# A two-layer graph network on one core: block bases loaded one per slice, packs of the next block in its free places, indices of the small group kept, and chunks 0 to 3 ahead of the last two

## The chip, the cores and the metric

The kernel runs on one core of a Trainium2 chip. The metric is the device time of one execution in microseconds (us), the median over several. The cores have these engines: TensorE (PE in the profile; PEld are its weight loads), VectorE (DVE), ScalarE (ACT), GpSimd (POOL) and SyncE (SP), which here only issues DMAs. A "q" behind an engine's name is its sequencer.

## The reference

There are 12500 nodes with 128 features, and 200000 edges, sorted by their destination `dst`, with a random source `src` and 64 edge features. Small destinations are far more frequent than large ones.

```python
def _dmpnn_layer(x, src, dst, edge_attr, W_msg, Wih, Whh, bih, bhh):
    msg = jnp.concatenate([x[src], edge_attr], axis=-1) @ W_msg.T
    agg = jax.ops.segment_sum(msg, dst, num_segments=n_nodes)
    return _gru_cell(agg, x, Wih, Whh, bih, bhh)

h = jnp.maximum(_layernorm(x, axis=-1), 0.0)
x = x + layer2(layer1(h))
```

`_gru_cell(m, h, ...)` makes r and z by sigmoids of two sums of matrix products, n by a tanh, and gives (1 - z) * n + z * h. All numbers are float32.

## The kernel before

**The edges.** They go in groups of 512 (128 partitions by 4 tiles): 390 full ones and a rest of 320 edges on 80 partitions, called the small group or the rest group. For a group, VectorE compares the destinations with a lane of numbers to make `onehot` (L1130), and TensorE multiplies it with the edge features (L786, in layer 0 only) and with the rows of the source nodes (L802), which gives sums for a window of 80 nodes in PSUM. VectorE adds the window to `edgeT` (L1192) and `aggT` (L1195), at a base that it reads from a table with a value load (L1187). `onehot` is made two places ahead.

**Two kinds of groups.** For 288 full groups and the rest, the source rows are gathered by GpSimd, four indirect DMAs of L666 a group, into a ring of six buffers. The first 102 groups have the smallest destinations. Their rows aren't gathered: TensorE builds count matrices out of one-hots (`lo_hot` L1108 and `v_hot` L1115, both of VectorE; matmuls of L755), ScalarE copies them to `a_blk` (L1385), and TensorE multiplies them with the resident node rows (L762) in seven slices. A count matrix of a slice is made in four packs.

**The block loop.** In each layer a loop of 12 blocks (`ITERS`) runs over 24 gathered groups (`gi` 0 to 23) in each block; in layer 0 every fourth place holds one dense group for its edge features alone, 32 places in all. Slice `sl` takes the groups 3 `sl` to 3 `sl` + 2, its phases 0 to 2. In phase 0 VectorE makes the one-hots of packs 2 and 3, in phase 2 those of packs 0 and 1 of the next slice, and in phase 2 of the last slice (`gi` = 20) those of packs 0 and 1 of the next block. In phase 1 of the last slice it prepares the next block. At `gi` = 21 TensorE turns the sums of the block's dense tiles into five short windows (L832), and `add_block` on VectorE reads five bases (L1217) and makes five adds (L1224).

**The chunks.** When all edges of 250 nodes are added, their GRU is computed as one of 50 chunks. The functions of L411 to L417 run the chunks that are ready behind `gi` = 5, 11 and 17 and behind the block's last place; L419 to L424 run all that are left behind the rest group. Both are loops at run time, with bounds that the kernel reads from a table. TensorE's part of a chunk is L866 to L895 (it begins with L875 and L879), ScalarE's L1418 to L1460, VectorE's L1269 to L1291. ScalarE also issues the chunk's DMAs: the store (L1420) and in layer 1 a load (L1448). `chunk_at` (L426) turns the place in the order into a chunk's number, computed in registers where it is used: on TensorE for L879, on ScalarE for L1420, L1429, L1448 (layer 1) and L1455 (layer 0). The order before is 4, 5, ..., 49, 0, 1, 2, 3, as the blocks' dense tiles reach into the nodes of chunks 0 to 3 until the last block; `late` makes these four ready at the very end. So chunk 48 is the last one in the loop, and 49, 0, 1, 2, 3 stand behind the rest group.

**What sets the order.** Each engine's program is written out; engines wait for each other by semaphores. SP issues the loads of edge features, destinations and indices in the order of use, each behind a wait for a free buffer (L513). Its load of the rest group's indices (L592) comes last in a layer. GpSimd's gathers of a layer begin when every row of its table is stored (L662). The registers' value loads are TENSOR_LOAD and FUSED_REGOPS in the profile.

```python
c = i + ROT - CHUNKS * ((i + ROT + 64 - CHUNKS) >> 6)
...
base = dve.value_load(base_i[0:1, bass.ds(g, 1)], min_val=0, max_val=N)
added_before(p)
dve.wait_ge(group_summed, p + (layer * ORDERED[0] + 1 + AHEAD))
...
starts = [dve.value_load(window_base[0:1, bass.ds(it * NR + r, 1)], min_val=0, max_val=N) for r in range(NR)]
```

Of the kernel before, what the change touches and what calls it, by code (L numbers as in the profile page):

```python
# [7 lines left out]
I32 = mybir.dt.int32  # L8
# [5 lines left out]
P = 128  # L14
# [18 lines left out]
SLOTS = SUBS * RING  # L33
ROT = 4
AR = 4
REGIONS = ((8, 2, 14), (7, 3, 20), (8, 4, 32), (7, 5, 36), (4, 6, 26))
# [14 lines left out]
def build(nc, x, src, dst, edge_attr, weights, h_table, x1_table, out):  # L51
# [5 lines left out]
    GROUPS = FULL + 1  # L57
    CHUNKS = N // CHUNK
    NT = N // QUART
    LN_STEPS = CHUNKS // LN_C  # L60
# [26 lines left out]
    with ctx:  # L87
# [28 lines left out]

        idx = sb("idx", [P, IDX_RING, RING, TILES], I32)
        dst_in = sb("dst_in", [P, AR, TILES], I32)
        rel = sb("rel", [P, 2, TILES])
# [56 lines left out]
        ones = start_only(P, 1)  # L176
        late = start_only(P, 1)
        need = start_only(P, 1)
# [73 lines left out]
        rows_loaded = [sem(f"rows_loaded{s}") for s in range(RING)]  # L252
        hr_loaded = [sem(f"hr_loaded{k}") for k in range(SUBS)]
        gather_issued = sem("gather_issued")
        dst_rows_loaded = sem("dst_rows_loaded")
# [114 lines left out]
        def idx_use(layer, it, gi):  # L370

            u, r = divmod(gi, RING)
            return it * (SUBS // IDX_RING) + u // IDX_RING + layer * (STEPS // IDX_RING + (u % IDX_RING == 0 and r == 0))

# [51 lines left out]
        def chunk_at(i):  # L426

            if isinstance(i, int):
                return (i + ROT) % CHUNKS
            c = i + ROT - CHUNKS * ((i + ROT + 64 - CHUNKS) >> 6)  # L430
            return nc.s_assert_within(c, 0, CHUNKS - 1,
                                      skip_runtime_bounds_check_because="a place plus ROT modulo the number of chunks")

# [62 lines left out]
        def _(sp):  # L496
# [54 lines left out]
            for layer in range(2):  # L551
# [3 lines left out]
                for gi in range(RING):  # L555
                    load_idx(0, gi)
                if layer == 0:
                    for p in range(AR):
                        load_edges(0, DENSE - HEAD + p, p)
                    for i in range(LN_STEPS):  # L560
                        sp.wait_ge(ln_relu, i + 1)
                        for a, b in PARTS:
                            sp.dma_start(by_node(h_table)[a:b, i * LN_C:(i + 1) * LN_C, :],
                                         hr_chunks(i * LN_C, (i + 1) * LN_C)[a:b]).then_inc(h_stored, 16)
                    for p in range(AR, HEAD):
                        slot_free(0, p)
                        load_edges(0, DENSE - HEAD + p, p % AR)
                else:
                    for q, gi, ai in order(layer)[:AR]:
                        load_group(layer, 0, q, gi, ai)  # L570
                    sp.wait_ge(out_stored, 16 * CHUNKS)
                    for k in range(SUBS):
                        first, last = ((slice_at[min(2 * i, SLICES)] + NQ - 1) // NQ for i in (k, k + 1))
                        for a, b in PARTS:
                            sp.dma_start(hr_chunks(first, last)[a:b],
                                         by_node(x1_table)[a:b, first:last, :]).then_inc(hr_loaded[k], 16)
# [14 lines left out]

                sp.dma_start(idx[0:REST, 0, 0, :], edges(src, FULL, REST)).then_inc(idx_loaded[0][0], 16)  # L592
                for k in range(2):
# [10 lines left out]
        def _(pool):  # L604
# [9 lines left out]
            nc.gpsimd.iota(bend[:, :], pattern=[[1, STEPS]], base=1, channel_multiplier=0, **small)  # L614
            nc.gpsimd.memset(late[:, :], float(STEPS + 1)).then_inc(late_made, 1)
            nc.gpsimd.memset(zero[:, :], 0.0)
# [17 lines left out]
            for r, (n, w, c) in enumerate(REGIONS):  # L634
                nc.gpsimd.affine_select(out=row_of[:, tiles_of(r)], in_=row_of[:, tiles_of(r)], compare_op=ALU.is_ge, fill=0.0,
                                        base=ROW_AT[r] + w - 1, pattern=[[w, n]], channel_multiplier=-1)
            pool.wait_ge(late_made, 1)
            nc.gpsimd.affine_select(out=late[:, :], in_=late[:, :], compare_op=ALU.is_ge, fill=0.0,
                                    base=-(CHUNKS - ROT - 1), pattern=[[0, 1]], channel_multiplier=1)
            pool.wait_ge(ident_zeroed, 1)  # L640
# [16 lines left out]
            for layer in range(2):  # L657
# [5 lines left out]

                def gather(s, i, parts):
                    for j in range(TILES):
                        nc.gpsimd.indirect_dma_start(  # L666
                            out=rows[0:parts, s, j, :], out_offset=None, in_=table[:, :],
                            in_offset=bass.IndirectOffsetOnAxis(ap=idx[0:parts, i, s, j:j + 1].bitcast(U32), axis=0),
                        ).then_inc(rows_loaded[s], 16)
# [7 lines left out]
                with pool.Fori(0, ITERS) as it:  # L677
                    for gi in range(SLOTS):
# [4 lines left out]
                        pool.sem_inc(gather_issued, 1)  # L683
                        gather(r, i, P)
                pool.wait_ge(group_summed, layer * ORDERED[0] + place(layer, ITERS, rows_free(0)) + 1 + AHEAD)
                pool.wait_ge(idx_loaded[0][0], (idx_use(layer, ITERS, 0) + 1) * 16)
                pool.sem_inc(gather_issued, 1)
                gather(0, 0, REST)

# [242 lines left out]
        def _(dve):  # L932
# [13 lines left out]
            for c in range(LN_STEPS + 1):  # L946
# [15 lines left out]
                if c >= 1:  # L962
# [37 lines left out]
            dve.wait_ge(consts_made, 1)  # L1000
            nc.vector.scalar_tensor_tensor(out=touch[:, :], in0=max_all[:, :], scalar=float(ROT * CHUNK),
                                           in1=gidx[:, :], op0=ALU.is_ge, op1=ALU.mult)
# [7 lines left out]
            chained(nc.vector.tensor_scalar(over[:, 0:1], over[:, 0:1], WIN - 0.5, None, ALU.is_ge))  # L1010
            chained(nc.vector.tensor_tensor(need[:, :], need[:, :], late[:, :], ALU.max))

# [110 lines left out]
            for layer in range(2):  # L1123
# [90 lines left out]

                def add_block(it, blk, p):

                    starts = [dve.value_load(window_base[0:1, bass.ds(it * NR + r, 1)], min_val=0, max_val=N) for r in range(NR)]  # L1217
                    added_before(p)
# [92 lines left out]
                with dve.Fori(0, ITERS) as it:  # L1311
                    blk = block_of(layer, it)
                    for q, gi, ai in order(layer):
                        g = it * ATTR + ai if gi is None else gathered(it, gi)
                        add_window(place(layer, it, q), g, slot(layer, q), P, gi is not None)
                        onehot_after(it, q)
                        if gi == USED:
                            add_block(it, blk, place(layer, it, q + 1))
                        if gi is not None and gi < USED:
# [6 lines left out]
                            elif phase == 2 and sl + 1 < SLICES:  # L1326
                                for k in range(2):
                                    pack_of(blk, sl + 1, k)
                            elif phase == 2:
                                for k in range(2):  # L1330
                                    lo_pack(it + 1, k)
                                    pack_of(blk + 1, 0, k)
                            elif sl == SLICES - 1:
                                prepare(it + 1)
                                nc.vector.tensor_scalar(v_onehot[:, :], lane[0:VC, :], vrel[:, bass.ds(it, 1)], None,
                                                        ALU.is_equal).then_inc(v_hot_made, 1)
# [173 lines left out]
```

## Time and profile before

| | |
|---|---|
| median of 3 runs | 3290.52 us (3289.2 to 3294.56) |
| the profiled execution | 3279.4 us, span 3277.7 us, mean granted TensorE clock 0.835 |
| layer 0: first and last gather | 73.0 to 1666.7 us |
| chunks behind the rest group of layer 0 | 1685.7 to 1718 us |
| layer 1: gathers | 1723.1 to 3221.7 us |
| chunks behind the rest group of layer 1 | 3238.8 to 3277.7 us |

Times are read from the start of the span. A row of a timeline gives start, duration, engine, line, operation, tiles and shapes, and in brackets how long the engine sat idle before it and what released it; "issue" is time in which it waited for nothing that the profile shows (its sequencer was at other instructions). A wait is listed with its sum, its count and its longest. The clock is given as a share of 2.4 GHz: 1.00 and 0.50 are the two levels.

### The profile page before, as it was taken

The numbers are of one execution on the slowest core, as the hardware profiler recorded it, in microseconds if no ns is written. First come the engines' busy times: TensorE is split into PE (matmuls) and PEld (weight loads), VectorE is DVE, ScalarE is ACT, GpSimd is POOL, SyncE is SP. The second block draws the span as 40 slices with busy tenths as digits, with TensorE's granted clock in tenths as the row PEclk, the third lists the DMA queues.
The fourth block names the chain that finished last, engine by engine and source line by source line (L and its number), as shares of the span: only waits on it lengthen the run. The fifth ranks groups of instructions, "written<-read, shape, count | busy, mean of one in ns | idle before, by whom it ended". The sixth has DMA issues, their size and how long they took to land.

```text
span 3277.7 us, 74395 instructions
## 1 busy us (share of the span) xinstructions
PE 2630.1 (80%) x20375; PEld 2360.7 (72%) x20376; DVE 1530.0 (47%) x4895; ACT 999.1 (30%) x2343; POOL 2324.6 (71%) x2389
## 2 busy tenths in 40 slices
PE   0689889899898898898975777787787787787887
PEld 0578778788787787787855676687677677686675
DVE  5544455454454544545443444444444445444444
ACT  5212223232232333332341222232232233333333
POOL 4477777777777776776717777777777777777772
PEclk9988798798798898988986777777787787887888
DMA  7233333333333333333315222222222222222221
GB/s 195 56 88 86 86 94 90 85 94 88 87 93 88 85 91 82 92 80 80 88 33 128 54 55 58 56 62 55 61 59 58 60 63 60 64 60 62 65 61 43
DMA packets 350922, 249.44 MB, mean 76 GB/s; under 512 B 226506, under 2 KB 312334, under 8 KB 350628
## 3 DMA queue, kind: packets, MB, share of 16 engines
q0 software_dynamic: 75232, 155.02, 17.5%
q1 hardware_dynamic: 254617, 70.47, 10.3%
q10 hardware_dynamic: 20779, 20.48, 2.1%
q8 instruction: 130, 2.13, 0.3%
q14 instruction: 164, 1.34, 0.1%
HBM read 226.51 MB, written 19.20 MB: 75 GB/s over the span
## 4 chain that ended last, share of the span: by engine, by line
PE 35%; POOL 30%; issue 16%; DVE 6%; DVEq 4%; DMA 3%; ACT 3%; ACTq 1%; SPq 1%; POOLq 1%
POOL rows L666 30%; PE ps_v L762 9%; PE ps_win L802 8%; PE ps_win L786 4%; PE ps_q L755 3%; DVEq L1187 2%; PE ps_c L755 2%; PE ps_b L879 1%; PE ps_b L880 1%; PE ps_d L866 1%; PE ps_d L895 1%; ACT hr L1366 1%; PE ps_a L886 1%; DVEq L1217 1%; PE ps_c L888 1%
## 5 line engine op out<-in xcount | busy, mean ns | idle before, releaser
L666 POOL DMA_INDIRECT rows<-h_table,idx x1156 | 1153.2, 998 | 485.3 <-issue 376.2
L666 POOL DMA_INDIRECT rows<-x_table,idx x1156 | 1144.5, 990 | 410.4 <-issue 402.1
L802 PE MATMUL ps_win<-onehot,rows 128*128 128x80 f32 x4624 | 743.3, 312 | 202.5 <-DMA rows<-x_table,idx 162.8
L802 PEld LDWEIGHTS ps_win<-onehot,rows 128*128 128x128 f32 x4624 | 663.7, 221 | 248.7 <-issue 145.9
L762 PE MATMUL ps_v<-hr,a_blk 125*128 125x128 f32 x4800 | 715.2, 319 | 0.0
L762 PEld LDWEIGHTS ps_v<-hr,a_blk 125*128 125x128 f32 x4800 | 698.4, 235 | 0.8
L1385 ACT COPY a_blk<-ps_q 125x224 f32<-125x224 f32 (+5 forms) x504 | 223.8, 480 | 856.3 <-PE ps_q L755 763.7
L1115 DVE SCALAR_TENSOR_TENSOR v_hot<-v_cur,lane 128x42 bf16<-128x42 f32 (+13 forms) x1180 | 435.1, 425 | 0.0
L786 PE MATMUL ps_win<-onehot,attr 128*64 128x80 f32 x3128 | 312.2, 253 | 120.2 <-DVE onehot L1130 80.4
L755 PE MATMUL ps_q<-v_hot,lo_hot 128*125 128x28 bf16 (+5 forms) x3696 | 289.4, 222 | 139.9 <-DVE v_hot L1115 117.7
L755 PEld LDWEIGHTS ps_q<-v_hot,lo_hot 128*125 128x125 bf16 x3696 | 272.5, 151 | 151.2 <-DVE v_hot L1115 128.9
L786 PEld LDWEIGHTS ps_win<-onehot,attr 128*64 128x64 f32 x3128 | 258.7, 149 | 158.0 <-DVE onehot L1130 77.8
L1195 DVE TENSOR_TENSOR aggT<-aggT,ps_win 128x80 f32 x578 | 133.0, 230 | 499.4 <-PE ps_win L802 436.7
L1130 DVE TENSOR_TENSOR onehot<-lane,rel 128x320 f32<-128x320 f32 x682 | 338.2, 496 | 23.4
L1192 DVE TENSOR_TENSOR edgeT<-edgeT,ps_win 64x80 f32 x391 | 89.6, 229 | 453.9 <-PE ps_win L802 286.6
L1385 ACT ACT_TABLE_LOAD x96 | 123.2, 1283 | 364.7 <-PE ps_q L755 348.4
L1280 DVE SCALAR_TENSOR_TENSOR r_sb<-ps_a,bT,r_sb 128x250 f32<-128x250 f32 x100 | 47.8, 478 | 362.5 <-ACT r_sb L1450 292.0
L1385 ACT COPY a_blk<-ps_c 125x70 f32<-125x70 f32 (+7 forms) x672 | 208.3, 376 | 15.1 <-PE ps_c L755 11.1
L755 PE MATMUL ps_c<-v_hot,lo_hot 128*125 128x70 bf16 (+3 forms) x2016 | 200.3, 244 | 6.5 <-DVE v_hot L1115 6.5
L755 PEld LDWEIGHTS ps_c<-v_hot,lo_hot 128*125 128x125 bf16 x2016 | 167.9, 158 | 11.8 <-DVE v_hot L1115 8.0
L1127 DVE TENSOR_SCALAR rel<-dst_in,base_all 128x4 f32<-128x4 int32 x682 | 163.5, 240 | 7.8 <-issue 6.4
L1442 ACT COPY h_ch<-ps_a 128x250 f32<-128x250 f32 x100 | 36.6, 366 | 383.7 <-PE ps_a L875 383.4
(191 smaller groups left out, 2038.3 us busy)
## 6 DMA issues: line engine op xcount, KB each, us to landing
attr<-in_edge_attr_dram SPq DMA_DIRECT2D x390, 128.0 KB
rows<-h_table,idx POOLq DMA_INDIRECT x1156
rows<-x_table,idx POOLq DMA_INDIRECT x1156
dst_in<-in_dst_dram SPq DMA_DIRECT2D x678, 2.0 KB
idx<-in_src_dram SPq DMA_DIRECT2D x576, 2.0 KB
x_table<-out_sb ACTq DMA_DIRECT2D x50, 125.0 KB
attr<-in_x_dram ACTq DMA_DIRECT2D x50, 125.0 KB
out_dram<-out_sb ACTq DMA_DIRECT2D x50, 125.0 KB
```

Of the source, the lines that this page charges most:

```text
L666: nc.gpsimd.indirect_dma_start(out=rows[0:parts, s, j, :], out_offset=None, in_=table[:, :], in_offset=bass.IndirectOffsetOnAxis(ap=idx[0: ...
L755: mm = nc.tensor.matmul((ps_q, ps_c)[k % 2][0:QUART, own], lo_hot[:, t + j, :], v_hot[:, k % 2, own], start=True, stop=True)
L762: mm = nc.tensor.matmul(ps_v[0:VC, 0:H], a_blk[:, t - slice_at[sl], :], hr[:, t, :], start=(t == 0), stop=(t == NT - 1))
L786: mm = nc.tensor.matmul(ps_win[r % 2][0:D, WIN:2 * WIN], attr[0:parts, r, j, :], onehot[0:parts, r % 2, j, :], start=(j == 0), stop=(j == ...
L802: mm = nc.tensor.matmul(ps_win[r % 2][:, 0:WIN], rows[0:parts, rr, j, :], onehot[0:parts, r % 2, j, :], start=(j == 0), stop=(j == TILES - 1))
L1115: ins = nc.vector.scalar_tensor_tensor(out=v_hot[:, k % 2, at].rearrange("p (t c) -> p t c", c=wide), in0=cur[:, t:t + n].unsqueeze(2).to_ ...
L1127: nc.vector.tensor_scalar(rel[:, s % 2, :], dst_in[:, s, :], float(N), base_all[:, bass.ds(g, 1)], ALU.min, ALU.subtract).then_inc(rel_rea ...
L1130: nc.vector.tensor_tensor(onehot[:, s % 2, :, :], lane[:, 0:WIN].unsqueeze(1).to_broadcast([P, TILES, WIN]), rel[:, s % 2, :].unsqueeze(2) ...
L1187: base = dve.value_load(base_i[0:1, bass.ds(g, 1)], min_val=0, max_val=N)
L1192: ins = nc.vector.tensor_tensor(e, e, ps_win[s % 2][0:D, WIN:2 * WIN], ALU.add)
L1195: ins = nc.vector.tensor_tensor(a, a, ps_win[s % 2][:, 0:WIN], ALU.add)
L1385: ins = nc.scalar.copy(a_blk[:, 0:hs, row:row + n * w].rearrange("p h (j w) -> p j h w", w=w), (ps_q, ps_c)[k % 2][0:QUART, at].rearrange( ...
```

## The change

The five bases of a block's windows are read one each in phase 1 of slices 0 to 4 and kept in registers until `add_block`. The one-hots of packs 0 and 1 of the next block are made behind groups 22 and 23, one pack each, where both stood behind group 20. The rest group's indices have a tile of their own, loaded once at the start, and GpSimd waits for that. Chunks 0 to 3 stand ahead of chunks 48 and 49: order 4, ..., 47, 0, 1, 2, 3, 48, 49. For that `early` and `cap` take the place of `late` in the small computation at the start that finds when a chunk is ready, and `chunk_at` has three shifts where it had one.

```diff
+LAST = 2
+    MOVED = CHUNKS - ROT - LAST
+        idx_rest = sb("idx_rest", [P, TILES], I32)
...
-            return it * (SUBS // IDX_RING) + u // IDX_RING + layer * (STEPS // IDX_RING + (u % IDX_RING == 0 and r == 0))
+            return it * (SUBS // IDX_RING) + u // IDX_RING + layer * (STEPS // IDX_RING)
...
         def chunk_at(i):
             if isinstance(i, int):
-                return (i + ROT) % CHUNKS
-            c = i + ROT - CHUNKS * ((i + ROT + 64 - CHUNKS) >> 6)
+                return i + ROT if i < MOVED else i - MOVED if i < MOVED + ROT else i
+            c = i + ROT - (MOVED + ROT) * ((i + 64 - MOVED) >> 6) + MOVED * ((i + 64 - MOVED - ROT) >> 6)
+            c = c - CHUNKS * ((i + 64 - CHUNKS) >> 6)
...
                 if layer == 0:
+                    sp.dma_start(idx_rest[0:REST, :], edges(src, FULL, REST)).then_inc(rest_loaded, 16)
                     for p in range(AR):
...
-                sp.dma_start(idx[0:REST, 0, 0, :], edges(src, FULL, REST)).then_inc(idx_loaded[0][0], 16)
...
-            nc.gpsimd.memset(late[:, :], float(STEPS + 1)).then_inc(late_made, 1)
+            nc.gpsimd.iota(cap[:, :], pattern=[[1, 1]], base=CHUNK, channel_multiplier=CHUNK, **small)
+            nc.gpsimd.memset(early[:, :], float(ROT * CHUNK)).then_inc(late_made, 1)
...
-            nc.gpsimd.affine_select(out=late[:, :], in_=late[:, :], compare_op=ALU.is_ge, fill=0.0,
-                                    base=-(CHUNKS - ROT - 1), pattern=[[0, 1]], channel_multiplier=1)
+            nc.gpsimd.affine_select(out=early[:, :], in_=early[:, :], compare_op=ALU.is_ge, fill=0.0,
+                                    base=MOVED - 1, pattern=[[0, 1]], channel_multiplier=-1)
...
-                pool.wait_ge(idx_loaded[0][0], (idx_use(layer, ITERS, 0) + 1) * 16)
+                pool.wait_ge(rest_loaded, 16)
                 pool.sem_inc(gather_issued, 1)
-                gather(0, 0, REST)
+                gather(0, idx_rest, REST)
...
-            nc.vector.scalar_tensor_tensor(out=touch[:, :], in0=max_all[:, :], scalar=float(ROT * CHUNK),
+            chained(nc.vector.tensor_scalar(cap[:, :], cap[:, :], float((CHUNKS - LAST) * CHUNK), None, ALU.max))
+            nc.vector.tensor_tensor(cend[:, :], cend[:, :], cap[:, :], ALU.min)
+            nc.vector.scalar_tensor_tensor(out=touch[:, :], in0=max_all[:, :], scalar=early[:, 0:1],
                                            in1=gidx[:, :], op0=ALU.is_ge, op1=ALU.mult)
...
-            chained(nc.vector.tensor_tensor(need[:, :], need[:, :], late[:, :], ALU.max))
...
-                def add_block(it, blk, p):
-
-                    starts = [dve.value_load(window_base[0:1, bass.ds(it * NR + r, 1)], min_val=0, max_val=N) for r in range(NR)]
+                def add_block(starts, blk, p):
+
...
                         if gi == USED:
-                            add_block(it, blk, place(layer, it, q + 1))
+                            add_block(starts, blk, place(layer, it, q + 1))
+                        if gi is not None and gi > USED and gi - USED <= 2:
+                            lo_pack(it + 1, gi - USED - 1)
+                            pack_of(blk + 1, 0, gi - USED - 1)
...
-                            elif phase == 2:
-                                for k in range(2):
-                                    lo_pack(it + 1, k)
-                                    pack_of(blk + 1, 0, k)
-                            elif sl == SLICES - 1:
+                            elif phase == 1 and sl < NR:
+                                starts.append(dve.value_load(window_base[0:1, bass.ds(it * NR + sl, 1)], min_val=0, max_val=N))
+                            elif phase == 1 and sl == SLICES - 1:
                                 prepare(it + 1)
```

## Rows read from the trace of the kernel before

**Rows 1.** The page: part 1, busy us and share; part 4, the chain by line.

```profile
PE 2630.1 (80%) x20375; PEld 2360.7 (72%) x20376; DVE 1530.0 (47%) x4895; ACT 999.1 (30%) x2343; POOL 2324.6 (71%) x2389
...
POOL rows L666 30%; PE ps_v L762 9%; PE ps_win L802 8%; PE ps_win L786 4%; PE ps_q L755 3%; DVEq L1187 2%; PE ps_c L755 2%; PE ps_b L879 1%; PE ps_b L880 1%; PE ps_d L866 1%; PE ps_d L895 1%; ACT hr L1366 1%; PE ps_a L886 1%; DVEq L1217 1%;
```

**Rows 2.** Windows: us from:to, length, busy of each engine, PEclk, DMA share, GB/s.

```profile
862.00:1662.00 800.00, 719.78 (x5911) 633.75 (x5910) 396.49 (x1269) 264.92 (x624) 570.31 (x575) 0.89 0.34 86
1723.00:3221.00 1498.00, 1162.19 (x8464) 1065.22 (x8464) 653.08 (x1932) 434.58 (x1004) 1143.85 (x1156) 0.78 0.26 63
1252.20:1262.40 10.20, 7.45 (x23) 5.10 (x24) 3.04 (x11) 1.11 (x3) 7.76 (x9) 0.50 0.25 67
854.00:862.00 8.00, 4.58 (x27) 4.04 (x28) 2.42 (x10) 0.00 (x0) 6.17 (x7) 0.64 0.37 90
```

**Rows 3.** Waits of PE, 1723 to 3221: us, times, longest.

```profile
PE ps_win L802 <- DMA rows<-x_table,idx: 162.8, 69, 16.7
```

**Rows 4.** Waits of PE, 862 to 1662.

```profile
PE ps_win L786 <- DVE onehot L1130: 42.4, 29, 5.1
PE ps_win L786 <- issue: 18.9, 6, 3.8
PE ps_q L755 <- DVE v_hot L1115: 5.2, 18, 0.5
PE ps_b L879 <- issue: 3.8, 19, 0.3
```

**Rows 5.** Instructions of L879, 862 to 1662: duration ns, first and last start.

```profile
L879 PE MATMUL ps_b<-aggT,wT x60: 374/473/782, 866.1 to 1641.0; 128*128 x60
```

**Rows 6.** Timeline of DVE, end of block 9: start, us, instruction, [idle before].

```profile
1240.47 2.04 DVE L1108 TENSOR_TENSOR lo_hot<-lane,lo_t 128x1000 bf16<-128x1000 f32 x2
...
1243.85 0.65 DVE L1115 SCALAR_TENSOR_TENSOR v_hot<-v_cur,lane 128x70 bf16<-128x70 f32 x2
...
1246.73 0.49 DVE L1130 TENSOR_TENSOR onehot<-lane,rel 128x320 f32<-128x320 f32 x1
1250.51 0.17 DVE L1224 TENSOR_TENSOR aggT<-aggT,ps_v 128x14 f32 x1 [3.28 <-issue]
...
1256.20 0.23 DVE L1192 TENSOR_TENSOR edgeT<-edgeT,ps_win 64x80 f32 x1 [0.40 <-issue]
```

**Rows 7.** Instructions of L1217: duration ns min/median/max.

```profile
L1217 DVEq FUSED_REGOPS  x240: 57/132/190, 228.6 to 3221.1; - x120
L1217 DVEq TENSOR_LOAD <-edgeT x120: 298/300/318, 228.8 to 3220.7; - x120
```

**Rows 8.** Timeline of PE, end of block 9.

```profile
1254.21 1.33 PE L786 MATMUL ps_win<-onehot,attr 128*64 128x80 f32 x8 [5.11 <-DVE onehot L1130]
...
1256.93 1.20 PE L879 MATMUL ps_b<-aggT,wT 128*128 x2
...
1273.18 1.32 PE L786 MATMUL ps_win<-onehot,attr 128*64 128x80 f32 x8 [3.77 <-issue]
```

**Rows 9.** Timeline of POOL, end of layer 0.

```profile
1662.19 0.91 POOL L666 DMA_INDIRECT rows<-h_table,idx  x1 [13.36 <-DMA idx<-in_src_dram]
```

**Rows 10.** Timeline of PE, end of layer 0.

```profile
1680.64 1.12 PE L802 MATMUL ps_win<-onehot,rows 80*128 80x80 f32 x8
1685.68 0.65 PE L875 MATMUL ps_a<-ident,h_rows 125*128 125x125 f32 x2 [3.92 <-issue]
```

**Rows 11.** Instructions of L1420: duration ns min/median/max.

```profile
L1420 ACTq FUSED_REGOPS  x98: 172/184/193, 306.8 to 3268.5; - x98
```

**Rows 12.** Timeline of all engines, around a chunk in mid-block.

```profile
1201.74 0.47 ACT L1457 ACTIVATE z_sb<-ps_d,b_gate 128x250 f32<-128x250 f32 x1 [0.19 <-PE ps_d L895]
...
1205.64 0.28 PE L786 MATMUL ps_win<-onehot,attr 128*64 128x80 f32 x1 [0.57 <-DVE onehot L1130]
```

**Rows 13.** Timeline of PE, end of layer 1.

```profile
3264.22 0.69 PE L895 MATMUL ps_d<-m_sb,wT 128*128 128x250 f32 x2 [0.23 <-ACT r_sb L1450]
```

**Rows 14.** Waits of all engines, 3221 to 3278.

```profile
PE ps_b L879 <- DVE aggT L1195: 5.7, 1, 5.7
```

More of the change, by code:

```diff
@@ L176, in build @@
         ones = start_only(P, 1)
-        late = start_only(P, 1)
+        early = start_only(P, 1)
+        cap = start_only(P, 1)
         need = start_only(P, 1)
@@ L253, in build @@
         hr_loaded = [sem(f"hr_loaded{k}") for k in range(SUBS)]
+        rest_loaded = sem("rest_loaded")
         gather_issued = sem("gather_issued")
@@ L428, in chunk_at @@
             if isinstance(i, int):
-                return (i + ROT) % CHUNKS
-            c = i + ROT - CHUNKS * ((i + ROT + 64 - CHUNKS) >> 6)
+                return i + ROT if i < MOVED else i - MOVED if i < MOVED + ROT else i
+            c = i + ROT - (MOVED + ROT) * ((i + 64 - MOVED) >> 6) + MOVED * ((i + 64 - MOVED - ROT) >> 6)
+            c = c - CHUNKS * ((i + 64 - CHUNKS) >> 6)
             return nc.s_assert_within(c, 0, CHUNKS - 1,
-                                      skip_runtime_bounds_check_because="a place plus ROT modulo the number of chunks")
+                                      skip_runtime_bounds_check_because="the first ROT chunks stand behind all but the last LAST")
         def edges(a, g, parts):
@@ L662, in _, with gather @@
                     pool.wait_ge(out_stored, 16 * CHUNKS)
-                def gather(s, i, parts):
+                def gather(s, at, parts):
                     for j in range(TILES):
@@ L667, in gather @@
                             out=rows[0:parts, s, j, :], out_offset=None, in_=table[:, :],
-                            in_offset=bass.IndirectOffsetOnAxis(ap=idx[0:parts, i, s, j:j + 1].bitcast(U32), axis=0),
+                            in_offset=bass.IndirectOffsetOnAxis(ap=at[0:parts, j:j + 1].bitcast(U32), axis=0),
                         ).then_inc(rows_loaded[s], 16)
@@ L683, in _ @@
                         pool.sem_inc(gather_issued, 1)
-                        gather(r, i, P)
+                        gather(r, idx[:, i, r, :], P)
                 pool.wait_ge(group_summed, layer * ORDERED[0] + place(layer, ITERS, rows_free(0)) + 1 + AHEAD)
-                pool.wait_ge(idx_loaded[0][0], (idx_use(layer, ITERS, 0) + 1) * 16)
+                pool.wait_ge(rest_loaded, 16)
                 pool.sem_inc(gather_issued, 1)
-                gather(0, 0, REST)
+                gather(0, idx_rest, REST)
                 def over_gather(g, parts, sent, n, done):
@@ L1312, in _ @@
                     blk = block_of(layer, it)
+                    starts = []
                     for q, gi, ai in order(layer):
```

## The prediction

> **What bounds the kernel now.** I read the page first: TensorE is busy 80% of the span and GpSimd 71% [rows 1], so no engine bounds the whole. Next the windows by stage. From 862 to 1662 us, the second half of layer 0, TensorE's records fill 719.8 of 800 us; from 1723 to 3221, the groups of layer 1, they fill 78% of it while GpSimd is busy 1143.85 of 1498 us in 1156 transfers [rows 2]. The list of waits then says what ends TensorE's idle time. In layer 1 it is the gathered rows, 162.8 us [rows 3]: there GpSimd's pace sets the time. In 862 to 1662 no wait for rows is in the list. What is there is 42.4 us for `onehot` (longest 5.1), 18.9 us of "issue" (the jump back of the block loop, up to 3.8 each time), 5.2 us for `v_hot` in 18 waits and 3.8 us before L879 in 19 [rows 4]. So in blocks 6 to 11 of layer 0 every microsecond that TensorE loses or gains is one of the end. Those are six block ends, 30 chunks (60 matmuls of L879, two per chunk [rows 5]), 18 of them the first of a step in mid-block, six the first at a block end, six the second of a step.
>
> A profiled execution took 3279.4 us against a median of 3290.5, 11.1 less; the sum is made on the profiled one and its difference laid on the median. A measurement of this kernel tells about 0.2%, 6.6 us, from no change.
>
> **Part A and B, the block's end.** [Rows 6] are VectorE's records of one. At gathered group 20 (counted from 0) two packs take it from 1240.47 to the end of the `v_hot` of 1243.85, some 3.95 us. Then `onehot` at 1246.73, then 3.28 us of idle under "issue" before the first add of L1224: the five value loads of L1217. One load holds the sequencer 0.71 us: a TENSOR_LOAD of 0.30, register instructions of 0.06 and 0.19, the gaps between them [rows 7]; five make 3.55. TensorE waits 5.11 us for the onehot behind them, and its chunk, L879 at 1256.93, begins 0.73 after VectorE's last add at 1256.20 [rows 6, 8]. Moved to phase 1 of slices 0 to 4, each load lies in idle time of VectorE (busy half the stretch [rows 2]), and I cost it at nothing; were that cover gone, the five would cost 3.55 again. The packs, 3.95 us, are not saved: they stand behind the onehots of groups 22 and 23 instead, 2.6 and 1.35, still ahead of the last add. With the onehots first, TensorE's wait of 5.1 shrinks to about 0.8, and VectorE makes packs while TensorE multiplies the last groups; but the last add, and with it L879, still waits for all of VectorE's work. So of that path the 3.28 us go, and about 0.8 come back where VectorE waits for the matmuls of the last groups: gain 2.5 us an end, bounds 1.5 (if more comes back) and 3.3 (nothing does). Six ends in the bound stretch: **−15 us** (−9 to −20). The next block's first matmuls come at 1273.18 [rows 8], 16 us later, so the packs are not late. In layer 1 and in blocks 0 to 5 rows are waited for: nothing.
>
> **Part C, the rest's indices.** The load moves to the start, one more DMA on SP there, beside hundreds of loads. GpSimd no longer waits for it at the end of a layer; in layer 0 that wait is 13.36 us [rows 9]. Its first transfer goes at 1662.19 [rows 9]; TensorE takes the group at 1680.64, behind chunk 48 [rows 10]. Nothing, bounds 0 and −1.
>
> **Part D, the order.** Before: chunk 48, rest group, then chunks 49, 0, 1, 2, 3. After: 0, 1, 2, 3, 48, rest group, 49. Six chunks either way behind the last group, one jump of 3.9 us either way [rows 10], one chunk at the low clock ahead of it and one behind. SP loads layer 1's attributes when the rest group is summed, now some 20 us later; the first gather of layer 1 needs every chunk stored and comes later still. Nothing by itself, bounds ±2. The one more iota and one more small VectorE instruction at the start run before the turned tiles arrive: nothing.
>
> **What D costs: the chunk's index.** A chunk's number is computed from a loop register wherever it is used. Before this is one FUSED_REGOPS with one shift, 184 ns on ScalarE's L1420 [rows 11]; after it has three shifts, four multiplications and about eight sums. The shortest of L1217, a multiply and two sums, take 57 ns [rows 7], so the shift and two cheap operations more are 127 ns, most of it the shift. Two more shifts at about 0.1 and eight cheap operations at about 0.01 give an extra δ of 0.27 us for each use. Bounds: 0.1 if only the cheap ones count, 0.4 if the whole triples. I take 0.27, as the row with the same operations is nearest.
> How often is it on the path? [Rows 12] show a chunk in mid-block. TensorE computes it before L879 (+δ). ScalarE computes it before its store L1420, then its L1450, then before the copies L1429 and L1455: these stand one behind the other on its sequencer, so L1457 moves by 4δ less its slack of 0.19, then VectorE's last three operations, its next value load, add and onehot, and TensorE, which already waits 0.57 us for that onehot. So a first chunk in mid-block costs 4δ − 0.19 = 0.89, 18 times: 16.0. The six second chunks cost about 2δ, 3.2; the six at block ends δ, 1.6. Sum **+21 us** in the stretch.
> The tails: six chunks of layer 0's end at δ, +1.6. In layer 1's end TensorE waits for ScalarE's L1450 before L895 [rows 13], behind two DMAs each with its index: 2δ for four chunks and δ for the two at the low clock, +2.7; its block end, where L879 waits 5.7 us for the adds [rows 14], gives back 1.5.
> As layer 0 saturates a little earlier and layer 1's last blocks wait for rows by under 1 us, +2.
>
> Sum: −15 + 20.8 + 1.6 + 2.7 − 1.5 + 2 = **+10.6**, 3290.0 on the profiled execution, **3301 us** on the median. In δ: 106δ − 3.4 − 14.5; nothing is gained or lost at δ = 0.17, a gain over 6.6 us needs δ under 0.11.
>
> The row of a TENSOR_LOAD is 0.30 us and its whole load 0.71 [rows 7]. The Trainium skill (Runtime: NRT & Kernel Launch, "Instruction fetch mechanics") puts such a load at about 200 ns for each register; by that five loads would be 1.0 us, A would give little, and the sum would be near +24. The trace disagrees with it here, as the idle time that it ends is 3.28.
>
> **Rivals.**
> 1. The index is cheap, δ = 0.1. For it: the added operations are mostly sums and products. Against: the one shift seems the dear part. Then 106δ = 10.6, and the sum is −7.3: 3283 us, faster. It decides from δ under 0.11. Chance 0.17.
> 2. The clock. After the 5.1 us stall TensorE stood at 0.50 for 10.2 us with 7.45 us busy [rows 2], the 1.2 GHz level. If a stall of 0.8 plus one of 3 us keeps 2.4 GHz, half of the 7.45 goes at six ends, −22 us: 3279 us. Against: TensorE still idles some 3.6 us in all before L879, and shorter waits at 856 us were also followed by a low clock (0.64 in the mean of 854 to 862 [rows 2]). Chance 0.12.
> 3. Neither is on the path: GpSimd's transfers pace layer 0 too, and its slack takes both. Then only the tails remain, +3: 3293 us. Against: no wait for rows after 862. Chance 0.12.
> 4. The moved packs and loads hit a busy VectorE: the gain is 0 to 1 an end instead of 2.5: +20 to +25, 3312 us. Chance 0.09.
> 5. D does not do what it says: chunks 0 to 3 don't become ready before the last groups and the order is as before. The time would be that of the forecast, since D by itself is worth nothing.
>
> **How the numbers follow.** The forecast, with δ between 0.2 and 0.35, has 0.50; its own range is 3294 to 3308. The range from 3276 to 3312 takes in rivals 1, 3 and most of 2. Faster by over 0.2% is below 3283.9: rival 2 and half of rival 1, with spread 0.24. Slower is above 3297.1: most of the forecast and rival 4, 0.50. The same: 0.26.
>
> **What would show it.** Idle before L1224 falls from 3.28 to under 0.3 and the five value loads stand one each at gathered groups 1, 4, 7, 10 and 13; TensorE's longest wait for onehot in a block falls from 5.1 to about 1, with a new wait before L879 of about 3 us; FUSED_REGOPS of L1420, L1429, L1448, L1455 and L879 grow from 0.18 to 0.45; the wait for onehot after a mid-block chunk grows from 0.57 to about 1.4; layer 1's chunks behind the rest group come about 0.5 us further apart. FUSED_REGOPS still under 0.3, or a clock of 1.00 behind the block end, would make the forecast wrong.

## The result

The changed kernel takes 3308.08 us in the median of 7 executions (3296.66 to 3321.07), the kernel before 3289.2 in 7 beside it (3279.99 to 3294.56). The ratio is 1.0067, with a 95% interval of 1.0052 to 1.0083: by that 22 us slower (the two medians differ by 19), where 10.6 were forecast, and 3308 against a forecast of 3301 in a range of 3276 to 3312. Single executions of one kernel lie up to 25 us apart. The profiled one of the changed kernel took 3321.07 us, 13 above its median, while the one of before was 11 below its own. So the two traces differ by 42 us where the kernels differ by 22, and a trace is read here for what a step does, not for the total.

The profile page of the changed kernel, its first part and the row of the granted clock:

```profile
PE 2669.9 (80%) x20375; PEld 2392.0 (72%) x20376; DVE 1530.4 (46%) x4896; ACT 1011.6 (30%) x2343; POOL 2336.5 (70%) x2390
...
PEclk9988888898798897888986677787787787787887
```

The same 20375 matmuls take 40 us more than in [rows 1]. No matmul was added, and the mean granted clock is 0.824 where it was 0.835, which is about that much. The waits of TensorE from 862 to 1690 us (the same six blocks as in [rows 4], which take longer here):

```profile
PE ps_win L793 <- DVE onehot L1138: 20.7, 24, 1.1
PE ps_b L886 <- DVE edgeT L1200: 20.2, 6, 3.6
PE ps_win L793 <- issue: 19.5, 6, 3.7
PE ps_b L886 <- issue: 10.8, 24, 0.6
PE ps_a L882 <- issue: 7.0, 6, 1.2
PE ps_q L762 <- DVE v_hot L1123: 4.5, 13, 0.5
```

Beside [rows 4] the wait for `onehot` has fallen from 42.4 us to 20.7 and its longest from 5.1 to 1.1. In its place stands a new wait of up to 3.6 us, 20.2 in all, at the six block ends, where L886 (L879 before) waits for the last add, and the "issue" in front of L886 has grown from 3.8 to 10.8 us. VectorE at the end of block 9, first, TensorE, second, and third TensorE's first row there in the kernel before:

```profile
1264.37 0.49 DVE L1138 TENSOR_TENSOR onehot<-lane,rel 128x320 f32<-128x320 f32 x1
1264.78 0.16 DVE L1231 TENSOR_TENSOR aggT<-aggT,ps_v 128x14 f32 x1
...
1268.33 2.04 DVE L1116 TENSOR_TENSOR lo_hot<-lane,lo_t 128x1000 bf16<-128x1000 f32 x2
...
1271.88 0.87 DVE L1116 TENSOR_TENSOR lo_hot<-lane,lo_t 128x125 bf16<-128x125 f32 x2
1272.67 0.64 DVE L1123 SCALAR_TENSOR_TENSOR v_hot<-v_cur,lane 128x70 bf16<-128x70 f32 x2
1273.23 0.22 DVE L1200 TENSOR_TENSOR edgeT<-edgeT,ps_win 64x80 f32 x1
```

```profile
1263.45 0.43 PE L839 MATMUL ps_v<-v_onehot,v_rows 128*128 128x128 f32 x2
...
1268.47 0.77 PE L793 MATMUL ps_win<-onehot,attr 128*64 128x80 f32 x8 [1.10 <-DVE onehot L1138]
1270.33 0.40 PE L882 MATMUL ps_a<-ident,h_rows 125*128 125x125 f32 x2 [1.09 <-issue]
1274.32 1.20 PE L886 MATMUL ps_b<-aggT,wT 128*128 x2 [3.58 <-DVE edgeT L1200]
```

```profile
1243.92 0.43 PE L832 MATMUL ps_v<-v_onehot,v_rows 128*128 128x128 f32 x2
```

The first add has no idle time in front of it; in [rows 6] it was 3.28 us. But both packs now stand between the block's adds and the last add, and TensorE waits for that. From the block's own matmul (L839) to L886 it is 10.87 us; before it was 13.01, from 1243.92 to the 1256.93 of [rows 8].

The index of the store on ScalarE, which was one FUSED_REGOPS of 184 ns in [rows 11]:

```profile
L1429 ACTq FUSED_REGOPS  x294: 42/184/223, 305.6 to 3309.5; - x147
```

There are three for each of the 98 stores: one of about 184 ns, one of about 218 and one of about 48. From a store's first register instruction to its DMA it is 0.351 us before and 0.599 here, in the median of the 98. So the δ of the prediction is 0.25. TensorE's register instructions have no records, but its idle time in front of the chunk's L886 grew from 0.17 to 0.44. All engines around a chunk in mid-block, and under them the first matmul of the chunk of [rows 12] in the kernel before:

```profile
1206.41 0.38 PE L882 MATMUL ps_a<-ident,h_rows 125*128 125x125 f32 x2
1207.23 0.68 PE L886 MATMUL ps_b<-aggT,wT 128*128 x2 [0.44 <-issue]
...
1211.97 0.47 ACT L1466 ACTIVATE z_sb<-ps_d,b_gate 128x250 f32<-128x250 f32 x1
...
1213.84 0.42 DVE L1298 TENSOR_TENSOR z_sb<-m_sb,r_sb 128x250 f32<-128x250 f32 x1
...
1215.99 1.25 PE L793 MATMUL ps_win<-onehot,attr 128*64 128x80 f32 x8 [0.85 <-DVE onehot L1138]
```

```profile
1196.87 0.38 PE L875 MATMUL ps_a<-ident,h_rows 125*128 125x125 f32 x2
1197.41 0.68 PE L879 MATMUL ps_b<-aggT,wT 128*128 x2 [0.17 <-issue]
```

L1466 no longer waits for TensorE: ScalarE's own sequencer is late. From the chunk's first matmul (1206.41) to L793 it is 9.58 us; before, it was 8.77 (1196.87 to the 1205.64 of [rows 12]). TensorE's wait for the onehot behind it is 0.85 us; the prediction had 1.4. And then something follows that the kernel before doesn't show here. Windows of the changed kernel, and under them those of the kernel before, at about the same place: the second of each pair begins some 0.5 us behind the start of L793 (0.4 behind that of L786 before). The clock is the third number from the end:

```profile
1206.00:1215.00 9.00, 8.55 (x69) 6.71 (x67) 2.24 (x6) 3.21 (x9) 6.87 (x8) 1.00 0.31 81
1216.50:1226.50 10.00, 10.00 (x59) 9.59 (x58) 5.45 (x19) 2.14 (x7) 7.56 (x9) 0.51 0.30 75
```

```profile
1197.00:1206.00 9.00, 8.27 (x69) 6.55 (x68) 3.02 (x8) 4.16 (x9) 6.87 (x8) 1.00 0.34 95
1206.00:1216.00 10.00, 9.73 (x98) 9.06 (x97) 6.29 (x22) 2.47 (x8) 7.56 (x9) 1.00 0.31 78
```

Behind a wait of 0.85 us TensorE fell to 1.2 GHz for 10 us and did 59 matmuls in a stretch that held 98 before, behind a wait of 0.57.

### The profile page after: what moved, and what is told of

It is laid out like the page before. It is cut to its first block, busy times and chain, and to the rows that moved or that the text cites. A ratio compares the mean times of both kernels' runs of the same rounds, so it can differ in the third digit from the quotient of the medians.

```text
span 3319.4 us, 74786 instructions
## 1 busy us (share of the span) xinstructions
PE 2669.9 (80%) x20375; PEld 2392.0 (72%) x20376; DVE 1530.4 (46%) x4896; ACT 1011.6 (30%) x2343; POOL 2336.5 (70%) x2390
## 4 chain that ended last, share of the span: by engine, by line
PE 41%; POOL 25%; issue 15%; DVE 6%; ACT 3%; DMA 3%; ACTq 3%; DVEq 2%; SPq 1%; POOLq 0%
POOL rows L673 25%; PE ps_v L769 12%; PE ps_win L809 10%; PE ps_win L793 5%; PE ps_q L762 3%; PE ps_c L762 2%; PE ps_b L886 2%; PE ps_b L887 2%; DVEq L1195 2%; ACTq L1429 1%; PE ps_d L873 1%; DMA rows<-x_table,idx 1%; ACT hr L1375 1%; DVE v_hot L1123 1%; PE ps_a L893 1%
## 5 line engine op out<-in xcount | busy, mean ns | idle before, releaser
L809 PE MATMUL ps_win<-onehot,rows 128*128 128x80 f32 x4624 | 753.8, 315 | 195.6 <-DMA rows<-x_table,idx 157.4
L809 PEld LDWEIGHTS ps_win<-onehot,rows 128*128 128x128 f32 x4624 | 674.1, 224 | 241.9 <-issue 124.8
L769 PE MATMUL ps_v<-hr,a_blk 125*128 125x128 f32 x4800 | 723.4, 321 | 0.0
L769 PEld LDWEIGHTS ps_v<-hr,a_blk 125*128 125x128 f32 x4800 | 706.5, 237 | 0.7
L793 PE MATMUL ps_win<-onehot,attr 128*64 128x80 f32 x3128 | 313.5, 253 | 79.4 <-DVE onehot L1138 45.3
L793 PEld LDWEIGHTS ps_win<-onehot,attr 128*64 128x64 f32 x3128 | 259.6, 149 | 116.2 <-issue 59.7
L1135 DVE TENSOR_SCALAR rel<-dst_in,base_all 128x4 f32<-128x4 int32 x682 | 165.3, 242 | 10.6 <-issue 9.1
```

What stands on the lines that cost most here:

```text
L769: mm = nc.tensor.matmul(ps_v[0:VC, 0:H], a_blk[:, t - slice_at[sl], :], hr[:, t, :], start=(t == 0), stop=(t == NT - 1))
L793: mm = nc.tensor.matmul(ps_win[r % 2][0:D, WIN:2 * WIN], attr[0:parts, r, j, :], onehot[0:parts, r % 2, j, :], start=(j == 0), stop=(j == ...
L809: mm = nc.tensor.matmul(ps_win[r % 2][:, 0:WIN], rows[0:parts, rr, j, :], onehot[0:parts, r % 2, j, :], start=(j == 0), stop=(j == TILES - 1))
L1135: nc.vector.tensor_scalar(rel[:, s % 2, :], dst_in[:, s, :], float(N), base_all[:, bass.ds(g, 1)], ALU.min, ALU.subtract).then_inc(rel_rea ...
```

## The experiments

Twelve kernels in three groups of four, each group on another chip. Each ratio is to the kernel before, run beside them on the same chip; 0.1% is 3.3 us, and the difference of two ratios is good to between 0.2 and 0.3%. The letters are those of the prediction.

| kernel | ratio to before | interval |
|---|---|---|
| changed kernel | 1.0067 | 1.0052 to 1.0083 |
| changed kernel again | 1.0084 | 1.0067 to 1.0102 |
| index as a value (same program) | 1.0098 | 1.0077 to 1.0118 |
| D undone: A, B, C | 0.9949 | 0.9930 to 0.9968 |
| the same, index as a value (same program) | 0.9955 | 0.9940 to 0.9971 |
| before with the two-shift index | 1.0052 | 1.0033 to 1.0071 |
| A, B, C with the two-shift index | 1.0023 | 1.0005 to 1.0040 |
| A, B, C with the three-shift index | 1.0067 | 1.0046 to 1.0088 |
| changed order, index kept in registers | 1.0018 | 1.0001 to 1.0034 |
| A, B, C, index kept in registers | 0.9978 | 0.9962 to 0.9994 |
| changed kernel with B undone | 1.0012 | 0.9994 to 1.0029 |
| before with B alone | 1.0050 | 1.0030 to 1.0071 |
| **before with A alone** | **0.9917** | 0.9903 to 0.9930 |

**Part D undone.** The order and the index of before, in the changed kernel:

```diff
-            c = i + ROT - (MOVED + ROT) * ((i + 64 - MOVED) >> 6) + MOVED * ((i + 64 - MOVED - ROT) >> 6)
-            c = c - CHUNKS * ((i + 64 - CHUNKS) >> 6)
+            c = i + ROT - CHUNKS * ((i + ROT + 64 - CHUNKS) >> 6)
...
-            nc.vector.scalar_tensor_tensor(out=touch[:, :], in0=max_all[:, :], scalar=early[:, 0:1],
+            nc.vector.scalar_tensor_tensor(out=touch[:, :], in0=max_all[:, :], scalar=float(ROT * CHUNK),
```

> The changed kernel with part D undone: the chunk order 4 to 49, 0 to 3, `late` and the one-shift index of before; A, B and C stay. Theory 1 (the longer index computation is the loss, A and B are a gain of 15 us in six block ends): 12 to 18 us below before, 3270 to 3278 where before is 3290, and 30 us or more below the changed kernel. Rival 2 (the moved packs and loads lose time themselves): at or above before, +0 to +10 us. Rival 3 (A and B gain nothing because the stall only moves to L879): within 4 us of before.

It took 3264.19 us against 3282.36, a gain of 0.51% or 17 us, where the steps of the prediction give 16.5 (15 and 1.5). So A, B and C together gain, D loses, and both signs of the sum stand.

**The longer index alone**, on the kernel before, with constants that keep the order:

```diff
-            c = i + ROT - CHUNKS * ((i + ROT + 64 - CHUNKS) >> 6)
+            c = i + ROT - CHUNKS * ((i + 64 - (CHUNKS - ROT)) >> 6) + (CHUNKS - ROT) * ((i + 64 - CHUNKS - 1) >> 6)
+            c = c - CHUNKS * ((i + 64 - CHUNKS - 1) >> 6)
```

> The kernel before with one edit: the index of a chunk is computed with three shifts as in the changed kernel, with constants that leave the order as it was. Theory 1: each use costs 0.27 us more, 106 of them weighted by the path are 25 us: 20 to 30 us above before, and more stretches of low TensorE clock behind chunks in mid-block, whose idle time grows by 0.3 to 0.8 us. Rival 2 (the new order itself costs, not the index): within 4 us of before. Rival 3 (the index costs only its own time, the rest of the loss is the clock of disturbed runs): +10 us or less.

17 us slower, 0.52%, where 20 to 30 were expected. The trace shows that this was a smaller dose than I meant: the last two shifts are the same, and one of them was dropped. The store's row of the kernel with this index and A, B, C has two FUSED_REGOPS for each store:

```profile
L1426 ACTq FUSED_REGOPS  x196: 172/195/202, 306.8 to 3268.2; - x196
```

From the first of them to the DMA it is 0.504 us, 0.15 more than before, for which the prediction's formula (106 δ − 3.4) gives 13 us. The low clock behind mid-block chunks that I expected to grow wasn't more in this execution (17 us against 20).

**The index computed once.** `pe.snap(chunk_at(i))` at the start of TensorE's chunk, three such values on ScalarE:

```diff
-                    c = chunk_at(i)
+                    c = pe.snap(chunk_at(i), min_val=0, max_val=CHUNKS - 1)
```

> The changed kernel, but a chunk's index is computed once for a chunk: on TensorE ahead of its transposes, on ScalarE the three that it needs right behind the first activation of the chunk, where its sequencer waits for the table load. Theory 1: the 4 delta on ScalarE's path go and one on TensorE stays, so the changed kernel's loss goes: 10 to 20 us below before. Rival 2 (order or moved packs cost): still 5 to 20 us above before.

> Both edits together: the order and index formula of before, the index computed once for a chunk, A, B and C kept. Theory 1: ScalarE's path is shorter than before by some 4 times 0.2 us in each mid-block chunk, so it lies 15 to 30 us below before and 3 to 10 us below the kernel with part D undone alone. Rival 3 (a mid-block chunk isn't on the path of TensorE): the same as with part D undone, within 3 us.

Both missed, 0.98% above and 0.45% below before. The traces show why: the FUSED_REGOPS stand at L1429, L1438 and L1465 as before, and none at the start of the chunk. The value was computed where it is used, and each engine has as many instructions as in the changed kernel and the one with D undone. The ratios are near theirs (0.98 beside 0.67 and 0.84% above; 0.45 beside 0.51% below). They say nothing on the path, but serve as repeats.

**Order or index?** Two kernels with the order of before and A, B, C; first the index with one shared shift, later one whose operations are those of the changed kernel one for one:

```diff
+            c = i + ROT - CHUNKS * ((i + 64 - (CHUNKS - ROT)) >> 6) + (CHUNKS - ROT - LAST) * ((i + 64 - CHUNKS - 1) >> 6)
+            c = c - CHUNKS * ((i + 64 - CHUNKS - 2) >> 6)
```

> A, B and C with the chunk order of before, but the index computed with three shifts. It differs from the changed kernel in the order alone. The changed kernel lies 1.2% above the one with part D undone, the longer index on the kernel before cost 0.5%. Theory 1a (the order is free, and the longer index costs more where A and B are in): 0.6 to 0.9% above before, as the changed kernel. Rival (the order itself costs some 20 us): within 0.2% of before, as -0.5 and +0.5 cancel.

> A, B and C, the order of before, and an index with the very operations of the changed kernel: three shifts in three FUSED_REGOPS. (The two earlier long indices shared one shift, so each use had two shifts and one instruction fewer, 0.16 us longer than before in the trace where the changed kernel's is 0.26.) It differs from the changed kernel in the order and the two start-up operations alone. Theory 1a (order free): as the changed kernel in the same call within 0.2%, 0.5 to 0.9% above before. Rival (the order costs 10 to 20 us itself): 0.3 to 0.6% below the changed kernel.

> The changed kernel itself, once more beside the others on one chip: 0.6 to 1.0% above before by what it and the run with the index as a value (the same instructions in the trace) gave.

The first took +0.23% and seemed to speak for a price of the order. The second has the three FUSED_REGOPS of the changed kernel:

```profile
L1426 ACTq FUSED_REGOPS  x294: 42/184/223, 306.7 to 3287.2; - x147
```

It took +0.67%, the changed kernel beside it +0.84%, with intervals that overlap. So the order is worth 6 us by this pair, and its intervals allow anything from nothing to about 15. Against the kernel with D undone, the three-shift index costs 0.67 + 0.51 = 1.18%, **39 us**. The formula gave 25. The two-shift index costs 0.23 + 0.51 = 0.74% there, 24 us, against 13.

**The index in registers of its own**, filled for the next chunk at the end of one:

```diff
+                    c = pe.snap(chunk_no, min_val=0, max_val=CHUNKS - 1)
...
+                    pe.reg_mov(chunk_no, chunk_at(i + 1))
...
+                    act.reg_mov(chunk_nos[2], chunk_at(i + 2))
```

> The changed kernel with its order, the chunk numbers kept in registers of their own that are filled for the next chunk at the end of one, so no index is computed on the path of a chunk. (Computed as a value at the start of a chunk, in the earlier runs, the arithmetic still stood at each use in the trace.) Theory 1a (order free): 0.5 to 1.0% below before, 40 us below the changed kernel. Rival (the order costs 20 us): within 0.3% of before.

> The same registers with the order of before and A, B, C. Theory 1: the one-shift index leaves the path as well, 72 times 0.18 us in mid-block chunks of the bound stretch: 8 to 15 us below the kernel with part D undone, 0.75 to 1.0% below before. Against the run with the new order and kept indices it gives the order's own price: 0 by theory 1a, 20 us by the rival.

With the new order this takes away 0.5 to 0.8% of the changed kernel's time, which again puts most of the loss on the index. It doesn't reach the gain I expected, and with the order of before it is slower than computing the one-shift index in place (0.22% below before against 0.51%). The chunk's path did get shorter: from its first matmul to the start of VectorE's last operation it is 6.45 us in the median of the mid-block chunks, 6.73 with D undone. So the computation at a chunk's end isn't free either; what it delays wasn't traced to its end. The pair differs by 0.40%, 13 us, beyond its intervals. Part of it can be the three shifts that one of them still computes; how much is the order isn't settled.

**A and B apart.** B alone on the kernel before, B undone in the changed kernel, A alone on the kernel before:

```diff
+                            elif phase == 1 and sl < NR:
+                                starts.append(dve.value_load(window_base[0:1, bass.ds(it * NR + sl, 1)], min_val=0, max_val=N))
```

> The kernel before with part B alone: the packs of the next block stand behind groups 22 and 23, the five value loads stay in front of the block's adds. By my path the packs only move within VectorE's work before the last add, so L879 gains little from B: 0 to -5 us of before; the wait of 5.1 us for the onehot falls to about 4. Rival (the gain of 17 us comes from B, as TensorE's stall for onehot is cut): 10 us or more below before.

> The changed kernel with part B undone: the packs of the next block stand behind group 20 again. B alone on the kernel before cost 0.5%. If B costs by itself (packs ahead of the last adds delay L879 more than they save): 0.3 to 0.6% below the changed kernel. If B costs only where the value loads still stand in front (both between the onehots), and gains with A: at or above the changed kernel, up to 0.2%. My sum said B moves TensorE's wait and saves nothing by itself.

> The kernel before with part A alone: one value load in phase 1 of slices 0 to 4. By my working the 3.28 us of idle in front of L1224 go at each block end; TensorE's wait for onehot falls from 5.1 to about 1.8 and the last add is 2.5 to 3.3 us earlier: 10 to 20 us below before, 0.3 to 0.6%. If A and B together were needed for the gain of 0.5%: within 0.2% of before.

B costs in every pair: 0.50% on the kernel before, 0.72% in the changed one (0.84 against 0.12), 0.33% beside A (0.51 against 0.83, with intervals that touch). A alone gains 0.83%, 27 us, more than I had for A and B together, and is the fastest of all: 3256.02 us against 3282.67. VectorE and then TensorE of that kernel at the end of block 9:

```profile
1240.41 0.49 DVE L1130 TENSOR_TENSOR onehot<-lane,rel 128x320 f32<-128x320 f32 x1
1240.82 0.16 DVE L1223 TENSOR_TENSOR aggT<-aggT,ps_v 128x14 f32 x1
...
1246.51 0.23 DVE L1192 TENSOR_TENSOR edgeT<-edgeT,ps_win 64x80 f32 x1 [0.45 <-issue]
```

```profile
1237.74 0.43 PE L832 MATMUL ps_v<-v_onehot,v_rows 128*128 128x128 f32 x2
1239.18 0.77 PE L786 MATMUL ps_win<-onehot,attr 128*64 128x80 f32 x8 [1.01 <-DVE onehot L1130]
...
1243.46 1.12 PE L802 MATMUL ps_win<-onehot,rows 128*128 128x80 f32 x8 [1.73 <-DMA rows<-h_table,idx]
...
1246.48 0.65 PE L875 MATMUL ps_a<-ident,h_rows 125*128 125x125 f32 x2 [1.19 <-issue]
1247.23 1.20 PE L879 MATMUL ps_b<-aggT,wT 128*128 x2
```

From L832 to L879 it is 9.49 us, where it was 13.01 before and 10.87 with B as well. The wait for the last add is gone: L879 starts 0.75 us behind L875, as it did before (0.77). Over the six ends of the bound stretch this kernel has 9.2 to 9.5 us at four of them and 7.7 and 12.4 at the others; with D undone it is 10.5 to 10.7 at all six, in the changed kernel 10.8 to 10.9.

A new limit shows in these rows: TensorE waits for gathered rows, 1.73 us here and 3.38 at the end that takes 12.4, in all 7.5 us in four waits from 862 to 1662. The traces of the kernel before and of the changed one above show none there, those of the others at most 6.5 us. In this execution GpSimd's pace takes part of what A gives.

The changed kernel with B undone has block ends of 8.0 to 9.6 us, 8.8 in the mean, as at this one:

```profile
1384.37 0.43 PE L839 MATMUL ps_v<-v_onehot,v_rows 128*128 128x128 f32 x2
...
1389.40 0.77 PE L793 MATMUL ps_win<-onehot,attr 128*64 128x80 f32 x8 [1.12 <-DVE onehot L1138]
1391.36 0.65 PE L882 MATMUL ps_a<-ident,h_rows 125*128 125x125 f32 x2 [1.19 <-issue]
1392.40 1.20 PE L886 MATMUL ps_b<-aggT,wT 128*128 x2 [0.39 <-issue]
```

So B lengthens a block end by 2.1 us in the changed kernel, by 1.3 on the kernel before (14.3 against 13.0), and by 1.0 beside A, whose mean of 9.6 holds the end of 12.4. The changed kernel with B undone also gives a second way to part the loss: against A alone it takes 0.12 + 0.83 = 0.95% more, 31 us, for D, with C in it.

The Trainium skill (Runtime: NRT & Kernel Launch, "Instruction fetch mechanics") gives about 200 ns for a register's load. By that figure, an estimate, five loads would be 1.0 us. The trace's TENSOR_LOAD is 0.30 us and its whole value load 0.71, and the run with A alone bears that out: with five of them out of the path all of the 3.28 us of idle before the first add is gone.

## Why the prediction was right, and where its terms were off

The direction and the paths of A and of the index held; B was wrong in the division, and the index was mis-sized. That the time lies in the range was in part luck: the change is 22 us, and 28 and 32 in the two repeats, two to three times the forecast of 10.6. By the repeats' ratios the kernel would take 3317 and 3321 us beside the 3289.2 of before, above the range's 3312.

**The bound stage**, TensorE in blocks 6 to 11, was right, though with A in place it is near GpSimd's pace (above). The stretch of these blocks, from one block's own matmul to the same six blocks on, took 807.0 us before, 788.4 with A alone, 787.5 and 802.9 in the two executions with D undone, and 827.8, 827.1, 814.7 and 812.7 in the four with the three-shift index.

**A and B, −16.5 with the tail:** measured −17 and −15. From L832 to L879 I had 13.01 − 2.5 = 10.5; it is 10.5 to 10.7. As a sum this step held, but its division was wrong. "The packs are not saved … of that path the 3.28 us go, and about 0.8 come back" put A at 2.5 us and B at nothing. A alone takes 3.5 us off, and B puts 1.0 to 2.1 back at each end. In the tail of layer 1, where I had −1.5 for both, it is 60.7 us from the last block's own matmul to the end before, 56.8 with A, 59.5 with both and 62.5 with B alone. Behind group 20 the packs delayed a onehot, and TensorE lost 1.01 us (at some ends nothing); behind groups 22 and 23 all of their 3.95 us stand between the block's adds and the last one, with TensorE waiting.
In layer 1 I had nothing for A and B. From its first block's own matmul to the last's it is 1375.4 us before and 1375.2 with A alone, but 1378.2 with B alone and 1379.0 and 1379.5 with A and B: B costs some 3 to 4 us there too, in single executions.

**C, nothing:** GpSimd's wait of 13.36 us for the indices is gone (it waits 4.27 us for TensorE in its place), and no run shows a gain. It wasn't tried alone.

**D's order, nothing:** 6 us by one pair, with overlapping intervals, and up to 13 by the other, so nothing to 13 us, where the bounds were ±2. The six chunks stand as told: 1696.6, 1708.0, 1714.1, 1720.0 and 1725.8 us, then the rest group, then the jump of 3.47 and the last one at 1736.6.

**D's index, +28.6 − 3.4 = +25:** the term that was mis-sized. It measures 39 us beside A, B and C, and 31 without B (there with C and the order in it). With an error of 7 to 9 us the first is clear of 25 and the second is not. δ was 0.25 where I took 0.27, so it was not the price of one use. The path through a mid-block chunk was right: from its first matmul to the start of VectorE's last operation the median is 6.73 us before and 7.42 after, 0.69 more, and the whole chunk above took 0.81 more, where 4δ − 0.19 gives 0.81. What I left out is twofold:
- Layer 1. I had the index hidden behind the gathers but for the tail. With three shifts the stretch named above takes 1379.3 us without B and 1382.8 to 1386.1 with it, 3 to 7 us more than the same with one shift (1375.2; 1379.0 and 1379.5); with two shifts it was 1385.9 on the kernel before. In it TensorE's waits for ScalarE's L1450 (L1459) grew from 19.6 to 33.2 us from 1850 to 3215 us.
- The clock, which may be the rest. The list of rivals had it as a gain: "if a stall of 0.8 plus one of 3 us keeps 2.4 GHz". With B in place it didn't: time at the low level behind the block ends is 167 us before and 157 with D undone. With the packs behind group 20 and A, some of it came: 140 us with A alone, 143 in the changed kernel with B undone. But the other side of the same mechanism, longer waits behind the mid-block chunks, stood in no term. Low-clock time in mid-block (more than 35 us behind a block's own matmul), summed over the bound stretch, is 72, 65, 41 and 31 us in the four executions with A, B, C and the three-shift index and 20, 7, 44, 31 and 27 in those with the one-shift index (before, D undone twice, A, B). The means are 52 and 26. At half speed 26 us cost about 13, which would fill what is missing. It is not shown: the other executions don't follow the index's length. There it is 17 and 7 us with two shifts, 41 with three and B undone, and 41 and 48 with the index in registers; and one program gave 7 and 44.

So A is −27, B +11, the index +39 and the order 0 to 6, beside a measured 22 to 32. That these add up is no check, as each is a step between neighbours of one chain; the other chain has A at −27, C and D at +31, and B at +24. Of the rivals, the cheap index fell (δ is 0.25), that neither is on the path fell, and the clock's gain came only in part where B is out. The fourth names a time near the measured one, but not its reason: A and B together did give 2.5 us at each end. What holds of it is that B costs.

## What to carry to other kernels

Index arithmetic in a loop at run time is work on the sequencer: count how often it is evaluated (here at least four times for each chunk), on which engines' path, and what its dearest operation is. Two more shifts in a formula, 0.25 us at each use, became 31 to 39 us of 3290. Move what only occupies a sequencer (value loads) into idle time, but don't put arithmetic that others don't wait for yet in front of an add that they do. Try the parts of a change one by one: here the first alone was worth 27 us, and the other parts turned it into a loss.

## What was not expected of the hardware

A value load takes 0.71 us of the sequencer, and five ahead of an add were the whole 3.28 us of idle. From a chunk index's first register instruction to the store's DMA it takes 0.35 us with one right shift, 0.50 with two and 0.60 with three, where an instruction with a multiply and two sums takes 0.057. TensorE's clock went to 1.2 GHz for 10 us behind a chunk with one wait of 0.85 us and another of 0.44, and stayed at 2.4 GHz behind one with 0.57 and 0.17. That the waits decide it isn't shown: how often it does so differs so much between executions of one program (7 and 44 us of low clock in 800) that a change of 0.5% can't be read from two traces.
